# A decoder layer on one core: the last two batches' expert slots by one-hot matmuls, and softplus, routing and scatters in another order

## What is computed

```
x = layernorm(x + lightning_attention(x))            # 16 heads, chunks of 128 tokens, rms norm, Wo
x = layernorm(x + ssm(ctx, gate=x))                  # conv, silu, softplus(dt), a scan over 512 steps with 16 states
logits = x @ router.T                                # 64 experts
topw, topi = top_k(softmax(logits), 8)
pos = (running count of each expert's tokens) - 1    # over all 2048 tokens in order, capacity 256 per expert
xe[expert, pos] = x[token]                           # gathered rows
ye = (silu(xe @ gate) * (xe @ up)) @ down
y[token] = sum over its experts of topw * ye[expert, pos]
x = layernorm(x + y)
```

## Time and profile before

| | |
|---|---|
| time, median of 3 runs | 1346.63 us (1346.26 to 1353.73) |
| the profiled execution | 1349.46 us, span 1347.6 us |
| busy share: PE, DVE, POOL, ACT | 85%, 82%, 74%, 63% |
| first scan to last scan (`mixers`) | from 51.4 to about 755 us |
| after the last scan, to the first gather | 755 to 805.4 us |
| experts, then the last norm | 805.4 to about 1310, then to 1347.6 us |

### The profile page before, as it was taken

How to read it: one execution, slowest core, us unless ns; L and a number is a source line. 1 busy time by engine, 2 the same in 40 slices (tenths; PEclk the granted TensorE clock), 3 DMA queues, 4 the chain that set the end, 5 groups by cost and what they waited for, 6 DMA issues and landing times. The chain is left out here.

```text
span 1347.6 us, 19321 instructions
## 1 busy us (share of the span) xinstructions
PE 1138.9 (85%) x6389; PEld 757.4 (56%) x6389; DVE 1100.1 (82%) x1536; ACT 853.8 (63%) x1536; POOL 1003.9 (74%) x796
## 2 busy tenths in 40 slices
PE   7489997898979779967887718999999999999950
PEld 2234443354424434433443418999999999999940
DVE  2379988989968799878798566998888989898846
ACT  5474585734756444847345326888878888888843
POOL 0778768777899997999988744777777777777644
PEclk9698887997889789878978658999999999999985
DMA  6525425323242432163133306999999999999978
GB/s 244 140 72 191 110 65 145 99 70 83 49 111 61 124 84 51 46 154 106 38 83 102 98 13 208 302 315 305 308 304 306 305 313 301 313 301 311 285 138 326
DMA packets 97490, 235.26 MB, mean 175 GB/s; under 512 B 20704, under 2 KB 21216, under 8 KB 96752
## 3 DMA queue, kind: packets, MB, share of 16 engines
q1 hardware_dynamic: 65648, 162.66, 39.5%
q0 software_dynamic: 31744, 71.37, 22.3%
HBM read 147.48 MB, written 52.94 MB: 149 GB/s over the span
## 5 line engine op out<-in xcount | busy, mean ns | idle before, releaser
L1226 DVE TENSOR_TENSOR_SCAN hst<-hst,dbu 128x512 f32<-128x512 f32 x256 | 299.2, 1214 | 97.1 <-POOL dbu L1035 71.8
L1035 POOL TENSOR_TENSOR dbu<-rep,bc 128x1024 f32<-128x1024 f32 x128 | 301.8, 2360 | 64.1 <-PE y_ps L396 35.3
L1642 POOL DMA_INDIRECT sum_rows<-ye,tokens x128 | 205.5, 1606 | 98.4 <-ACT ye L1721 75.6
L396 PE MATMUL y_ps<-dbu,cs 128*32 128x512 f32 x512 | 167.8, 741 | 70.3 <-DVE dbu L1232 62.6
L799 ACT ACTIVATE hst<-rep,small_sb 128x512 f32<-128x512 f32 x256 | 165.9, 685 | 56.8 <-DVE dbu L1232 51.5
L1634 POOL DMA_INDIRECT xe<-x_rows,tokens x128 | 150.6, 1176 | 61.4 <-issue 37.8
L434 PE MATMUL ring<-first_raw,xT 128*128 128x512 f32 x384 | 176.7, 604 | 0.5 <-DVE x2T L1314 0.5
L1232 DVE TENSOR_TENSOR dbu<-hst,bc 128x1024 f32<-128x1024 f32 x128 | 156.7, 1224 | 4.4
L1684 PE MATMUL low<-xh,w1h 128*128 128x256 f32 x512 | 150.5, 294 | 0.0
L1684 PE MATMUL low<-xh,w1l 128*128 128x256 f32 x512 | 145.3, 284 | 0.0
L1684 PE MATMUL low<-xl,w1h 128*128 128x256 f32 x512 | 145.2, 284 | 0.0
(11 more groups left out here) (198 smaller groups left out, 2680.0 us busy)
## 6 DMA issues: line engine op xcount, KB each, us to landing
first_raw<-in_gate_up SPq DMA_DIRECT2D x64, 768.0 KB, 9.8
rep<-made SPq DMA_DIRECT2D x256, 128.0 KB
second_raw<-in_down SPq DMA_DIRECT2D x64, 256.0 KB, 5.1
bc<-bc_rows SPq DMA_DIRECT2D x64, 128.0 KB, 3.2
second_raw<-in_down SPq DMA_DIRECT2D x64, 128.0 KB, 7.2
rows<-sum_rows SPq DMA_DIRECT2D x16, 512.0 KB, 8.9
sum_rows<-x2T SPq DMA_DIRECT2D x1, 4608.0 KB, 17.2
xT<-in_x_turned SPq DMA_DIRECT2D x16, 256.0 KB, 3.0
```

What stands on the lines that cost most here:

```text
L396: ins = pe.matmul(y_ps[rows, :], sel, dbu[:, n % WORK, g, :], start=(k == 0), stop=(k == QUADS - 1))
L1035: pool.tensor_tensor(dbu[:, n % WORK, :, :], rep[:, i % 2, :, 1, :], bc[:, k, 0, :].unsqueeze(1).broadcast_to([P, 2, T]), ALU.mult).then_i ...
L1226: dve.tensor_tensor_scan(h, h, dbu[:, n % WORK, i, :], 0.0, ALU.mult, ALU.add).then_inc(scanned, 1)
L1642: pool.indirect_dma_start(sum_dram[e % SUMS], bass.IndirectOffsetOnAxis(ap=tokens[:, e, j:j + 1], axis=0), ye[:, e % YE, j, :], None, comp ...
```

## The change

Two things are in one kernel.

**Slots.** The third batch (b = 2) is no longer scattered. Its slots and those of the fourth are turned into `tokens` in SBUF by one-hot matmuls: with s = slot + 127, h = s >> 7 and l = s & 127, one DVE operation marks column h - 1 and another column l for each of a token tile's eight choices (`make_hots`, 128x1024 in 16-bit floats), ACT multiplies the second by the token number (`number_lows`), PE sums eight products of 128x128 (`place_tokens`), and DVE adds the result to `tokens` (`add_slots`). For the third batch this is placed in the fourth batch's blocks 2 and 3, by `HOT_AT`; for the fourth it follows the last scan (`place_last`). The table of the first two batches is loaded, turned and added in the fourth batch's block 2. `experts` has `tokens` when it starts. `last_slots`, `split_slots` and the two loads are gone.

**Order.** In softplus the `+ 1` Identity moves up behind the Exp and the `- 1` Identity (`rounded`) gets a place of its own, so that the two Ln stand together. The gate of tile 2 moves from block 3 into the next batch's block 0, beside that of tile 3 (except in the last batch). `rate_experts` is cut in two, the next query projection moves behind it, and so does its copy on ACT. On POOL `rotate` of block 3 moves one unit later and `steps_of_u` up by one. `sends` spreads the scatters otherwise: none for the last two units of block 0, two a unit from unit 2 of block 2 on, none for the second half of block 3.

```diff
+HOT_AT = ((2, 1), (2, 4), (3, 0), (3, 3))
+def sends(last, c, k):
+    if c == 2:
+        return 2 if k >= 2 else 0
+    if c == 3:
+        return 2 if last else 1 if k < UNIT // 2 else 0
+    if c == 0:
+        return 1 if k < 6 else 0
+    return 2 if k >= UNIT - 2 else 1
...
                     sum_states(n + 1)
+                    for j in hots_due(n + 1, 3):
+                        place_tokens(j)
+                    if back and c == 1:
+                        turn_rows(b - 1, 0)
+                        turn_rows(b - 1, 1)
                     if c < NT - 1:
                         update_state(t)
                     mix_values(t)
                     if front:
                         project_context(b + 1, 1)
                     if back and c == 1:
-                        rate_experts(b - 1)
+                        rate_experts(b - 1, (0, 1))
 
                     sum_states(n + 2)
+                    if back and c == 1:
+                        rate_experts(b - 1, (2, 3))
-                    if more:
+                    if more and not (back and c == 1):
                         project(t + 1, "q")
...
             def logs(b, tiles):
-                for n, m in enumerate(tiles):
-                    act.activation(ln[m], acc[:, m, :], ACT.Ln, bias=1.0)
-                    act.activation(dtu_of(m), acc[:, m, :], ACT.Identity, bias=ones[:, 0:1]).then_inc(soft_steps, 1)
-                    act.wait_ge(soft_steps, done + 2 * n + 1)
-                    act.activation(dtu_of(m), dtu_of(m), ACT.Identity, bias=half_sb[:, NT:NT + 1]).then_inc(soft_steps, 1)
-                    act.wait_ge(soft_steps, done + 2 * n + 2)
-                    act.sem_inc(ln_ready, 1)
+                for m in tiles:
+                    act.activation(ln[m], acc[:, m, :], ACT.Ln, bias=1.0).then_inc(logged, 1)
...
-                        if c == NT - 1 and k == 6 and not last:
-                            steps_of_u(b + 1, 0)
                         if n + 1 < SLOT_COUNT * B:
                             inputs(n + 1)
...
+                        if k == 5 and c == NT - 1 and not last:
+                            steps_of_u(b + 1, 0)
-                        if k == 5 and t + 1 < NT * B:
+                        if k == (5 if c < NT - 1 else 6) and t + 1 < NT * B:
                             rotate(t + 1)
...
-            scatter(B - 2, sent, sent + 3)
             for j in range(NT):
                 row_root(j)
-            scatter(B - 2, sent + 3, NT * TOPK)
...
+            def make_hots(j, hots, count):
+                for h in range(2):
+                    ins = dve.tensor_tensor(hots[:, h, :, :], place_of[:, h, j, :].unsqueeze(1).broadcast_to([P, P, TOPK]),
+                                            count, ALU.is_equal)
+                ins.then_inc(hots_made, 1)
```

371 lines of the change are left out of this document (222 added, 149 removed).

## The result

| | before | changed |
|---|---|---|
| median, 10 runs each | 1348.44 us (1346.26 to 1353.73) | 1341.27 us (1331.59 to 1348.21) |
| ratio of the times, 95% interval | | 0.9931 (0.9903 to 0.996) |
| the profiled execution, its span | 1349.46, 1347.6 us | 1336.12, 1334.3 us |

One run of the changed kernel was disturbed (1684.37 us) and is not in its range. The change is worth 0.7%, some 9 us by the ratio (the two medians differ by 7.2); 1326 us and a clear gain were forecast. Two things are to be noticed ahead of any row. The profiled execution gained 13.3 us where 20.2 were forecast. And its own time is 5.2 us under the median of its kernel, whose times spread over 17 us, where those of before spread over 7. (In the later sessions of runs the kernel before spread over 8 to 13 us too, so the 17 against 7 is no firm difference.)

The account below looks back on a forecast made before the run. No single bound in the first half, DVE and POOL hand work to each other; PE bounds the experts. Terms sum to -20.2 from 1349.46, so 1329.3 profiled; the median, 2.8 us lower, gives 1326 us, range 1312 to 1342.

Parts of the forecast that it names:

- prologue: Before the first blocks: the first Ln now stands behind two more activations, +0.5 us.
- The routing order: Block 1, three times: query copy moved behind the Exp, logits split; -5.4 us in all, ends -7.5 and 0.
- The 2.50 us go: Block 1: the expert choice's 2.50 us wait for its Exp vanishes once ACT's query copy stands behind that Exp.
- the second half of the logits: Block 1 on PE: comes one `y_ps` sum (about 1 us) later, where `shift_logits` needs it; 0.7 us counted against the gain.
- other waits take the place of those removed: Rival for the order gains: half given back, 13.3 us of 26.5 remain, time 1340 us; chance 0.25.
- all four gains: The gains of order, 26.5 us: softplus in block 3, softplus in block 0, scatters of blocks 0 and 1, routing.
- Softplus: Shorter ACT stretch and earlier `steps_of_u`: -12.0 us in block 3 (three times), -4.3 in block 0 (four times).
- Scatters: Fewer in blocks 0 and 1 of batches 2 and 3, -4.8 us; six more in block 2 of batches 1 and 2, +2.0.
- One-hots: Batch 3: +9.5 us in blocks 2 and 3 (between +3 and +26), -5.7 from last scan to first gather.
- the rival: After the last scan: one-hots run at two elements a cycle, 0.69 us for 1.15, 3.7 us less, 1323; chance 0.24.
- The change of block: Between the DVE chain's end and the first gather: only this is left, taken as 3.3 us.
- Experts' stage: After the first gather: bound by PE, untouched by the change, should keep its length.

Follow-up runs that it names:

- again: The changed kernel, no edit, profiled and timed a second time; median 1340.08 us, ratio to before 0.9931.
- exp_first: Changed kernel with block 1's routing order on PE as before, only ACT's query copy still behind the Exp; median 1340.32 us, ratio 0.9916.
- route_old: Changed kernel with block 1's routing order on PE and ACT put back as before; median 1338.43 us, ratio 0.9924.
- soft_route_old: Changed kernel with routing and softplus orders as before, one-hots and new scatter places kept; median 1349.31 us, ratio 1.0007.
- fill_c2: route_old plus two useless constant matmuls on PE in batch 0's block 2, ahead of the attention's values; 1343.44 us, ratio 0.9948.
- slots_only: Changed kernel with softplus, gate, routing and scatter order put back, only the one-hot part left; median 1351.22 us, ratio 1.0021.
- light: exp_first with scatters of batches 1 to 3 placed otherwise: 18, 4, 6, 4 in blocks 2, 3, 0, 1; median 1337.1 us, ratio 0.9916.
- dense: Changed kernel with batch 3's one-hots in blocks 2 and 3 compared against a written-out 16-bit count; median 1337.77 us, ratio 0.9896.
- best_c: exp_first with best_b's one-hots and fills, fill_c2's fill, scatters 12, 6, 8, 6 in blocks 2, 3, 0, 1; 1330.66 us, ratio 0.9855.
- best_b: route_old with dense's counts, one-hots moved to units where POOL idles, and short PE fills after the last scan; 1332.45 us, ratio 0.9882.

## Why the prediction was wrong

It said 1326 us, likely faster by over 1%; it is 1341.3. The direction and the range held, the size did not. Of the 15.3 us, 6.9 are in the sum (-20.2 forecast, -13.3 in the profiled execution) and 8.4 lie between that execution and the median. The sum, held against the first profile of the changed kernel:

| us | forecast | measured |
|---|---|---|
| block 3, batches 0 to 2 | -12.0 | -11.5 |
| block 0, batches 1 to 3 | -2.1 | -5.5 |
| prologue, batch 0's blocks 0 to 2 | -1.7 | +2.5 |
| blocks 1 (routing and scatters) | -10.2 | -2.3 |
| block 2, batches 1 and 2 | +2.0 | +0.5 |
| batch 3, block 2 to last product | +9.5 | +8.8 |
| after it, to the first gather | -5.7 | -9.0 |
| from there to the end | 0 | +3.2 |

So even the -13.3 is smaller misses that partly cancel around one large one, in blocks 1.

**From the profiled execution to the median.** I took over that the median lies 2.8 us below the profile of before; that was from three times, and over ten it is 1.0. The changed kernel's median lies 5.2 above its profile. Its last block 1 takes 53 us in one execution and 59 in another, and the profile showed the short one; that this makes up the 5.2 is likely and not shown. One profile of before could not show it, since its blocks 1 had no second fall.

**The routing order (-5.4) is the step that failed.** It brought +0.9, give or take some 3. "The 2.50 us go" was right. What I named as late next, the second half of the logits behind one sum, was right in place and wrong in size: 0.7 us a block was counted; DVE waited 3.15, 1.88 and 5.13 us for the logits in the three blocks (7.74 for the last in again), of which only batch 1 had any before, 1.74. I had looked at what stands between two instructions on PE's queue, and not at the ring: the moved transposes fill two of its three slots, and PE stops for ACT, for 1.3 to 2.0 us in each block. In batches 1 and 2 of this profile that gap and the order are all that is seen, with the clock at 1.00; in batch 3 the clock also falls behind the gap, and logits run at half speed. And where the Exp wait was taken away without that (exp_first), POOL took the time back: the earlier trace rows had it busy for 50.7 of the 55 us, and it was waited for through the scatters' landing and through DVE operations that stretch beside `dbu`. So the rival "other waits take the place of those removed" was the right one for routing, by mechanisms that I had not listed. That its 1340 us is so near the 1341.3 is luck: it halves all four gains alike, where softplus kept most of its own and routing lost all.

**Softplus (-15.8 with the prologue) was right in mechanism and came to -11.2.** Block 3 gave 9.5 us in route_old against soft_route_old, and 11.5 with the scatters that left it (12.0 forecast); block 0 of batches 1 to 3 gave 3.7 and 5.5 (2.1 forecast). The difference is batch 0. There the scans wait for the projection's weights to land: ACT's scaling of them waited 7.31 us where it had waited 3.86, so 2 us of an earlier start bought nothing. And the shorter softplus lets PE run ahead in block 2, idle, and lose the clock, 1.7 us (fill_c2). Block 1 of batch 0 grew by 1.2 to 1.9 us too; why is open.

**Scatters (-2.8) came to -1.9.** In soft_route_old against slots_only the two fewer gave 0.7 us in batch 3's block 0 and 2.2 in the block 1 behind it, for the 2.4 forecast; in batch 2 the second fall hides what they gave. Six more in block 2 cost 0.9 and 0.1 us, until it is full (light).

**One-hots: +9.5 and -5.7 were forecast, +8.8 and -9.0 measured in the profiles** (slots_only +8.9 and -9.0). Between scans the forecast of 1.15 + 0.4 us each was close to the 1.67 measured. After the last scan the rival was right, with all operands 16-bit and written out they take 0.61 each, 4.9 in all for 9.2. The Trainium skill ("Vector Engine (DVE) Microarchitecture Reference", section 5.1) has both halves of this, that such operands let two results be made at a time and that one element read again and again does not, and the trace agrees: 0.61 with written-out operands, 1.23 with one that repeats a value, 0.69 for the same operation once that is written out (dense). Of the 4.3 us that this gave, 3.5 went again: PE's 32 slot matmuls take 7.65 us, DVE waits 5.47 for them, and what follows the one-hots takes 6.4 us where I had counted 2.9. The change of block gave 2.3 back, 1.0 us for the 3.3 that I took.

**Experts' stage**: forecast unchanged, and within its own spread it is (542.2 us before, 540.6 to 545.8 after).

## What to carry to other kernels

An engine whose clock can fall when it idles may lose by finishing early what it gained: look, in the windows, at the granted clock behind each gap that a change makes, and put a gap's price at the work that follows it at half speed. A moved instruction takes its place in the buffers too: count the ring slots held while it waits, not only the queue. And where one engine is busy for over nine tenths of a stretch, a wait removed on another is worth what the busy one can give; take a second profile of a changed kernel before explaining a few us of it.

## What the runs showed of the hardware

- The same program had TensorE's clock at 0.50 for 6.8 us or for 20.5 us in the same place with PE fully busy. The block took 53.2 and 58.9 us. A gap of PE of 1.98 us stood ahead of that fall; one of 1.84 in the batch before was followed by none.
- Useless matmuls in a gap of 2.06 us (1.88 us of them) kept the clock at 1.00 and shortened the block by 1.7 us (fill_c2); the next block took 1.7 more. With no gap there they made it 1.2 longer (best_c).
- Matmuls of 128x128 in 16-bit whose operands lie eight elements apart took 0.24 us each at the lower level of the clock (32 in 7.65 us) and no less at the upper one (8 in 2.06 us between the scans of the changed kernel, at 744 us); with adjacent operands the kernel before had 8 in 1.01 us at the lower one. Which of the two operands costs it was not tried.
- Beside POOL's work a pair of DVE operations of 0.69 us each took 4.16 (dense), and two of 0.42 in block 1 took 2.95 and 3.03. Moving the one-hots to units where POOL idles took the whole of it away (best_b).
